# Maxima of an attention stage's first 256 tokens taken head group by head group, on one Trainium2 core

## What is computed

```python
mk, mv = split(mem @ Wkv.T)                       # keys and values of the gathered rows
logits = einsum('bhld,bmd->bhlm', q_heads, mk) / sqrt(8)
attn = softmax(logits, axis=-1)                   # per head h, token l, over rows m
out = einsum('bhlm,bmd->bhld', attn, mv)
x = x + tanh(g_xattn) * (out @ Wc.T)
```

## Time and profile before

| | us |
|---|---|
| median of three executions | 337.15 |
| lowest, highest | 333.48, 337.73 |
| the profiled execution | 335.67 |
| its span | 333.9 |

### The profile page before, as it was taken

How to read it: one execution, slowest core, us unless ns; L and a number is a source line. 1 busy time by engine, 2 the same in 40 slices (tenths; PEclk the granted TensorE clock), 3 DMA queues, 4 the chain that set the end, 5 groups by cost and what they waited for, 6 DMA issues and landing times.

```text
span 333.9 us, 5318 instructions
## 1 busy us (share of the span) xinstructions
PE 291.1 (87%) x1781; PEld 214.3 (64%) x1781; DVE 190.1 (57%) x686; ACT 155.5 (47%) x333; POOL 78.7 (24%) x165
## 2 busy tenths in 40 slices
PE   5899979999986778869999888998889997888993
PEld 2688979999985335547777666664333433357993
DVE  4585555766888777888787868220211206725344
ACT  1665543555543014757676667686314120045640
POOL 3873135465545422000000001000023000244000
PEclk9999997999999987999999999999999999689998
DMA  7832553656200000029180000100001000011002
GB/s 204 284 110 93 182 180 135 206 197 213 90 22 12 16 8 20 1 82 332 13 247 0 6 0 3 36 2 2 0 3 36 0 0 3 7 40 21 14 2 63
DMA packets 18459, 24.09 MB, mean 72 GB/s; under 512 B 2120, under 2 KB 14986, under 8 KB 18426
## 3 DMA queue, kind: packets, MB, share of 16 engines
q1 hardware_dynamic: 16836, 20.39, 18.3%
q0 software_dynamic: 1184, 3.14, 4.1%
q10 hardware_dynamic: 406, 0.16, 0.2%
HBM read 12.62 MB, written 10.93 MB: 71 GB/s over the span
## 4 chain that ended last, share of the span: by engine, by line
PE 59%; DVE 17%; DMA 8%; issue 6%; ACT 4%; POOL 4%; SPq 0%; DVEq 0%; ACTq 0%; POOLq 0%
PE ps L1417 8%; PE ps L1472 7%; PE ps L1526 6%; DVE mx L1093 4%; PE ps L1504 4%; PE ps L1365 4%; PE ps L1367 3%; PE ps L1366 3%; PE ps L1326 3%; PE ps L1644 3%; DMA pair<-in_ctx_dram,at 3%; PE ps L1650 3%; PE ps L1673 2%; PE ps L1412 2%; DVE kv_nat L1084 2%
## 5 line engine op out<-in xcount | busy, mean ns | idle before, releaser
L937 DVE CUSTOM_DVE_ANT_0 kv_nat<-ps,gain 128x400 f32<-128x400 f32 (+1 forms) x64 | 36.3, 573 | 22.1 <-PE ps L1367 19.8
L1365 PE MATMUL ps<-shared,q_hi 128*128 128x400 f32 (+1 forms) x128 | 46.9, 367 | 2.0 <-DVE best L937 1.2
L697 ACT ACTIVATE gain<-ps 128x400 f32<-128x400 f32 (+1 forms) x64 | 32.3, 505 | 32.5 <-PE ps L1367 32.2
L1093 DVE TENSOR_REDUCE mx<-ps 128x1 f32<-128x384 f32 x84 | 40.9, 546 | 9.6 <-PE ps L1504 9.5
L1367 PE MATMUL ps<-shared,q_lo 128*128 128x400 f32 (+1 forms) x128 | 44.8, 350 | 0.0
L1366 PE MATMUL ps<-shared,q_hi 128*128 128x400 f32 (+1 forms) x128 | 44.7, 349 | 0.0
L803 ACT ACTIVATE kv_nat<-ps 128x512 f32<-128x512 f32 x72 | 39.3, 602 | 9.0 <-PE ps L1526 8.2
L1526 PE MATMUL ps<-q_rows,k_blk 128*128 128x256 f32 x192 | 39.9, 300 | 2.6 <-DVE mx L1084 1.7
L1526 PEld LDWEIGHTS ps<-q_rows,k_blk 128*128 128x128 f32 x192 | 31.5, 190 | 8.0 <-issue 2.9
L1504 PE MATMUL ps<-k_blk,q_rows 128*128 128x384 f32 x84 | 28.5, 365 | 1.5 <-DVE mx L1093 1.4
L609 POOL TENSOR_TENSOR rstd<-var_eps,minus_half 128x4 f32<-128x4 f32 x2 | 2.1, 1032 | 114.1 <-DVE var_eps L1124 114.1
(11 more groups left out here) (297 smaller groups left out, 509.8 us busy)
## 6 DMA issues: line engine op xcount, KB each, us to landing
m_rows<-kv_nat SPq DMA_DIRECT2D x48, 201.0 KB, 2.1
kv_nat<-in_ctx_dram SPq DMA_DIRECT2D x5, 640.0 KB, 9.6
ew_sb<-in_L_ffn_eW_dram SPq DMA_DIRECT2D x1, 2048.0 KB, 10.2
rw_sb<-in_L_ffn_rW_dram SPq DMA_DIRECT2D x1, 1024.0 KB, 5.4
x_sb<-in_x_dram SPq DMA_DIRECT2D x2, 256.0 KB, 3.9
xn_rows<-xn SPq DMA_DIRECT2D x2, 256.0 KB, 2.3
out_dram<-fin SPq DMA_DIRECT2D x4, 128.0 KB, 1.9
rw_sb<-in_L_ffn_rW_dram SPq DMA_DIRECT2D x1, 256.0 KB, 2.9
```

What stands on the lines that cost most here:

```text
L697: act.activation(gain[:, m % 3, 0:end - start], ps[:, b:b + end - start], ACT.Relu).then_inc(s_rl, 1)
L937: dve.tensor_tensor_reduce(out=m_all[b2][:, start:end], in0=ps[:, b:b + end - start], in1=gain[:, m % 3, 0:end - start], scale=1.0, scalar ...
L1093: dve.tensor_reduce(to, sc, AX.X, ALU.max).then_inc(s_p1u, 1)
L1365: pe.matmul(o, q_h, hi, start=True, stop=False)
```

## The change

The list of jobs starts with the 32 heads of tiles 0 and 1 in order of head group: group 0 of both tiles, then group 1 and so on. Each group has a turn of its own: two transposes of four columns each, tiles 0 and 1, into one bank, two VectorE instructions over 4 partitions by 256 columns, and two DMAs that write 4 partitions' rows of one group into `q_rows`. The first logits of group g wait for the rows of group g alone (`s_nmgroup`). The opening holds 10 jobs: four rises of two heads (group 0), and the group's turn behind the first of five more rises of two heads. The rest of tiles 0 and 1 are rises of one head between the logits, and of the later tiles every third head (`(GH * g + j) % 3 == 2`) is too. A rise of one head keeps both products, 192 columns each, in one bank (`rise_1` has three slots). A turn waits only for the jobs whose maxima it turns, and stands behind two jobs of the next tile (one, for group 0).

There are 129 jobs: 9 rises with 18 heads in the opening, 44 rises of one head and 66 plain ones in the loop, 4 group turns and 6 tile turns. `jobs_at` now has a date for each quarter: all jobs up to its turn are spread over the first 10 of the 12 steps before that quarter, and the last two have none. So steps 0 to 9 have 53 jobs, 12 to 21 have 34, 24 to 33 have 32, and steps 10, 11, 22 and 23 none. The router's weight loads come behind the fourth group's rows, `ew1` behind the second quarter's rows and `ew2` behind the third's.

```diff
-LEAD = 5
+LEAD = 4
@@ program
+        nmg_hi = shared[0:GH, 3 * TOK:4 * TOK]
+        nmg_lo = shared[0:GH, 4 * TOK:5 * TOK]
+        rise_1 = kv_flat[:, 16 * W:16 * W + 3 * W].rearrange("p (b k) -> p b k", b=3)
@@ max_jobs
+            units = [(i, g, j) for g in range(NG) for i in range(TQ) for j in range(GH)]
+            units += [(i, g, j) for i in range(TQ, NT) for g in range(NG) for j in range(GH)]
+            first = 0
+            while units:
+                i, g, j = units[0]
+                key = -1 - g if i < TQ else i
+                w = together if first == 0 or len(jobs) < first + LEAD else 1
+                if jobs and key != owner:
+                    turn, mine = owner, 0
+                owner = key
+                jobs.append((i, (g, j, j + w)))
+                units, mine = units[w:], mine + 1
+                if turn is not None and mine == (1 if key == -2 else 2):
+                    jobs.append((turn, None))
+                    first = first or len(jobs)
+                    turn = None
@@ by_rise
-            return max_jobs(T)[m][1] is not None and m < opening_of(T)
+            i, unit = max_jobs(T)[m]
+            return unit is not None and (m < opening_of(T) or T <= 4 and (i < TQ or (GH * unit[0] + unit[1]) % 3 == 2))
@@ jobs_at
-            first, last = opening_of(T), (NQ - 1) * NG * T - 2
+            per, turns = NG * T, max_turns(T)
+            due = [opening_of(T)] + [turns[q] for q in range(1, NQ)]
...
-                return first + -(-(len(max_jobs(T)) - first) * min(x + 1, last) // last)
+                q, r = divmod(x + 1, per)
+                if q >= NQ - 1:
+                    return due[-1]
+                return due[q] + -(-(due[q + 1] - due[q]) * min(r, per - 2) // (per - 2))
@@ minus_max_rows (SyncE)
+                for g, done in enumerate(group_turns(T)):
+                    sp.wait_ge(s_p1u, done)
+                    for r, src in ((3 * DH, nmg_hi), (3 * DH + 1, nmg_lo)):
+                        sp.dma_start(q_rows[r:P:RS, g, 0:W].bitcast(F32), src[:, g * W:(g + 1) * W].bitcast(F32)
+                                     ).then_inc(s_nmgroup[g], 16)
@@ rise_of (ScalarE)
+                    elif by_rise(T, m):
+                        act.wait_ge(s_p1, m + 1)
+                        w, b = T * P // 2, job_bank(T, m) * HALF
+                        act.activation(rise_1[:, m % 3, 0:w], ps[:, b:b + w], ACT.Relu).then_inc(s_p1r, 1)
@@ max_job (VectorE)
+                    if unit is not None and by_rise(T, m) and m >= opening_of(T):
+                        dve.wait_ge(s_p1r, rises_before(T, m) + 1)
+                        g, j0, j1 = unit
+                        b = job_bank(T, m) * HALF + hk
+                        dve.tensor_tensor_reduce(out=rise_1[:, m % 3, 0:hk], in0=ps[:, b:b + hk], in1=rise_1[:, m % 3, 0:hk],
+                                                 scale=1.0, scalar=LOWEST, op0=ALU.add, op1=ALU.max,
+                                                 accum_out=mx[:, i, NG * j0 + g:NG * j0 + g + 1]).then_inc(s_p1u, 1)
...
+                    elif i < 0:
+                        c, b = slice((-1 - i) * W, -i * W), job_bank(T, m) * HALF
+                        link(dve.tensor_scalar(nmg_hi[:, c], ps[0:GH, b:b + W], -1.0, None, ALU.mult))
+                        dve.scalar_tensor_tensor(out=nmg_lo[:, c], in0=ps[0:GH, b:b + W], scalar=-1.0,
+                                                 in1=nmg_hi[:, c].bitcast(F32), op0=ALU.mult, op1=ALU.subtract
+                                                 ).then_inc(s_p1u, 1)
@@ max_job (TensorE)
-                        pe.wait_ge(s_p1u, m if m == len(jobs) - 1 else m - 1)
+                        pe.wait_ge(s_p1u, done_for(T, m))
+                        if i < 0:
+                            b = job_bank(T, m) * HALF
+                            for k in range(TQ):
+                                mine = mx[:, k, :].rearrange("p (j g) -> p j g", j=GH)[:, :, -1 - i]
+                                last = pe.transpose(ps[0:GH, b + k * P:b + (k + 1) * P], mine, ident[:])
+                            last.then_inc(s_p1, 1)
+                            return
...
+                    if by_rise(T, m) and m >= opening:
+                        b = job_bank(T, m) * HALF
+                        for k, keys in enumerate((kd_blk, k_blk)):
+                            last = pe.matmul(ps[:, b + k * hk:b + (k + 1) * hk], q_rows[:, g, i * P:(i + 1) * P],
+                                             keys[:, j0, 0:hk], start=True, stop=True)
+                        last.then_inc(s_p1, 1)
+                        return
@@ attention_pe
+                            if q == 0 and t == 0:
+                                pe.wait_ge(s_nmgroup[g], 32)
+                            elif s == 0:
                                 pe.wait_ge(s_nmrow[q], 32)
```

More of the change, by code:

```diff
@@ L285, in program @@
         s_p1 = sem("logits_for_max_ready"); s_p1u = sem("logits_for_max_used")
+        s_nmgroup = [sem(f"minus_max_row_of_group{g}") for g in range(NG)]
         s_nmrow = [sem(f"minus_max_row{L}") for L in range(NQ)]
@@ L331, in max_jobs, with done_for, group_turns @@
         def max_jobs(T):
[L334 to L343, removed]
-            return jobs + [(NT - 1, None)]
+            jobs, turn, mine, together = [], None, 0, 2 if T <= 4 else 1
+            units = [(i, g, j) for g in range(NG) for i in range(TQ) for j in range(GH)]
[14 more added lines that the diff above has]
+                    turn = None
+            return jobs + [(NT - 1, None)]
+        def done_for(T, m):
+            jobs = max_jobs(T)
+            i = jobs[m][0]
+            mine = [k for k, (tile, unit) in enumerate(jobs) if unit is not None and
+                    (tile == i if i >= 0 else tile < TQ and unit[0] == -1 - i)]
+            return max(mine) + 1
+        def group_turns(T):
+            return [max_jobs(T).index((-1 - g, None)) + 1 for g in range(NG)]
         def opening_of(T):
-            return max_turns(T)[0] + LEAD
+            return group_turns(T)[0] + LEAD
         def by_rise(T, m):
-            return max_jobs(T)[m][1] is not None and m < opening_of(T)
+            i, unit = max_jobs(T)[m]
+            return unit is not None and (m < opening_of(T) or T <= 4 and (i < TQ or (GH * unit[0] + unit[1]) % 3 == 2))
         def places(T, m):
@@ L376, in max_turns @@
             jobs = max_jobs(T)
-            return [jobs.index((TQ * (q + 1) - 1, None)) + 1 for q in range(NQ)]
+            return {q: jobs.index((TQ * (q + 1) - 1, None)) + 1 for q in range(1, NQ)}
         def jobs_at(T, step):
-            first, last = opening_of(T), (NQ - 1) * NG * T - 2
+            per, turns = NG * T, max_turns(T)
+            due = [opening_of(T)] + [turns[q] for q in range(1, NQ)]
             def upto(x):
-                return first + -(-(len(max_jobs(T)) - first) * min(x + 1, last) // last)
+                q, r = divmod(x + 1, per)
+                if q >= NQ - 1:
+                    return due[-1]
+                return due[q] + -(-(due[q + 1] - due[q]) * min(r, per - 2) // (per - 2))
             return range(0 if step < 0 else upto(step - 1), upto(step))
@@ L421, in _, with load_weights @@
                                  m_all[i % 2][:, c * STEP:c * STEP + CHUNK]).then_inc(s_mst[i], 16)
-            def minus_max_rows(T):
-                for q, done in enumerate(max_turns(T)):
+            def load_weights(q):
+                if q == 0:
+                    sp.dma_start(rw1_sb[:], rW1).then_inc(s_w, 16)
+                    sp.dma_start(rw2_sb[:], rW2.rearrange("(k p) n -> p k n", p=P)).then_inc(s_w, 16)
+                    sp.wait_ge(s_rz, 1)
+                    sp.dma_start(rw3_sb[:, :, 0:E], rW3.rearrange("(k p) n -> p k n", p=P)).then_inc(s_w, 16)
+                if q == 1:
+                    sp.dma_start(ew1_sb[:], eW1.rearrange("e c h -> c e h")).then_inc(s_w, 16)
+                if q == 2:
+                    sp.dma_start(ew2_sb[:], eW2.rearrange("e (k p) c -> p e k c", p=P)).then_inc(s_w, 16)
+            def minus_max_rows(T):
+                for g, done in enumerate(group_turns(T)):
[3 more added lines that the diff above has]
+                                     ).then_inc(s_nmgroup[g], 16)
+                load_weights(0)
+                for q, done in max_turns(T).items():
                     sp.wait_ge(s_p1u, done)
@@ L768, in rise_of @@
                 def rise_of(m):
-                    if by_rise(T, m):
+                    if by_rise(T, m) and m < opening_of(T):
                         act.wait_ge(s_p1d, rises_before(T, m) + 1)
@@ L1078, in max_job @@
                     dve.wait_ge(s_p1, m + 1)
-                    if unit is not None and by_rise(T, m):
+                    if unit is not None and by_rise(T, m) and m >= opening_of(T):
[5 more added lines that the diff above has]
+                                                 accum_out=mx[:, i, NG * j0 + g:NG * j0 + g + 1]).then_inc(s_p1u, 1)
```

(1 more changed line is left out.)

10 lines of the change are left out of this document (1 added, 9 removed).

## The result

The changed kernel takes 353.35 us (median of 4, 349.17 to 353.72) against 336.6 for the kernel before in the same runs: ratio 1.0529, 95% interval 1.0478 to 1.0581. The prediction was 339.4 us with a range up to 345.0. The direction was right and the size was not: 17 us slower instead of 3. All ratios here compare fast executions only, with executions of the kernel before that ran beside each set (its medians there were 335.7, 335.5 and 334.2 us), so a ratio can't be had by dividing two medians.

What follows compares the result with a forecast made beforehand. VectorE was taken to bound the loop and opening. Terms -7.6 + 10.9 - 1.4 + 2.1 - 0.9 = +3.1, say +3.0, on 335.67 gave 338.7; half the median's 1.5 excess made 339.4 us, range 334.5 to 345.0.

Steps and rivals of the forecast that it cites:

- its terms for the way over ScalarE: Loop rises: round trips take steps 0 to 3 to 11.0 us; in steps 4 to 9 each rise loses 0.1.
- The opening, -7.6: Before the first logits: 9 pairs and one turn instead of 22 and two, logits at 141.0 not 148.6 us.
- The term for the row DMAs: End of the opening: rows land 2.5 to 3.4 us behind the turn's last instruction, at 140.7 to 141.4.
- VectorE: 0.28 instead of 0.476: Loop: a rise of one head between logits takes VectorE 0.28 us, where a plain job takes 0.476.
- The round trip binds: Rival, chance 0.20: steps 0 to 3 take 12.2 us, each later rise loses 0.2; 344.0 or 344.7 us.
- 1.2 us of pause at a weighing: Loop stages: each takes its VectorE work plus 1.2 us of pause, with 4.1 as the floor.
- Steps 0 to 3, 11.0 forecast: First stage of the loop: 11.0 us instead of 6.5, +4.5, taken nearer to the round trip.
- the two bounds, 9.1 and 12.2: Steps 0 to 3: VectorE's work plus pause gives 9.1 us, the round trip of the rises gives 12.2.
- -1.4 for both: Steps 10 to 12 and 22 to 24: nearly the floor, 4.3 us instead of 5.0 each.
- +2.1 - 0.9: Steps 13 to 21 and 25 to 33: +2.1 us of VectorE work; six tile turns that wait less credit -0.9.
- Not slower: Rival, chance 0.25: round trip costs nothing, weighing pause is filled; steps 0 to 9 take 23.6 us, total 334.8 or 335.5.
- The prediction's last sign: Stages 13 to 33: if they also grow by more than 1 us each, the loop price of a rise is wrong.

Runs made afterwards that it cites:

- changed, clock kept: Changed kernel plus nine products of 512 columns into an unused bank while TensorE waits for the first group's rows; 349.83 us, ratio 1.0449.
- no loop rises, clock kept: Changed kernel with all jobs behind the opening plain, plus nine products into an unused bank before the first logits; 347.66 us, ratio 1.0377.
- 33 jobs: Kernel before with a longer opening, 30 pairs of heads and three turns instead of 22 and two; 332.5 us, ratio 0.9945.
- groups, long opening: Changed kernel's group order and group turns, but 22 pairs in the opening, no rises behind it, jobs spread evenly; 335.18 us, ratio 1.005.
- 29 jobs: Kernel before with a longer opening, 26 pairs of heads and three turns instead of 22 and two; 333.86 us, ratio 0.9984.

## Why the prediction was wrong

**How the 18.3 us divide.** By the sums of the tables: 93.91 (changed) to 91.26 (changed, clock kept) is 2.6 us for the clock; to 86.90 (no loop rises, clock kept) is 4.4 for the 44 rises; to 83.38 is 3.5 for 14 heads and two turns of the first block in the loop and not in the opening (that run had some half clock, so it is rather a little more); to 77.20 is 6.2 for the dates and for six more pairs, twelve heads, that belong in the opening (the expectation above says six heads); to 75.59 is 1.6 for the group turns. Dates alone were 4.6 on the kernel before, rises alone 4.8. The opening's 7.2 us are inside these net figures: steps 0 to 3 by themselves took 7.8 more than before.

**How the error of 15.2 us divides.** The forecast had +3.1 for this stretch. Put 0.476 for every 0.28 in its loop terms, take its terms for the way over ScalarE out, and it has +8.1 with all loop jobs plain; so it gave the rises -5.0. Measured at full clock, it is +11.3 with all jobs plain and +4.4 for the rises. That makes 9.4 us of error on the rises, 3.2 on the rest (1.9 of it in steps 10 to 12 and 22 to 24, below) and 2.6 on the clock. So the step that failed is the price of a rise between logits, on VectorE and behind a weighing.

**The opening, -7.6: right.** Measured -7.2. The term for the row DMAs had 2.5 to 3.4 us and they took 3.1. (From 145.38 to 148.60 it is 3.2; the 3.4 is a slip, and the 141.4 worked out with 3.2 is right.) The logits came at 139.66 and not at 141.0, mainly because this execution's first rise was 1.8 us earlier (131.71, 133.47 before).

**"VectorE: 0.28 instead of 0.476" for a rise between logits: wrong, and the largest error.** The figure was read where 44 heads follow each other in pairs. Between reductions a rise takes 0.45 (one and two plain jobs every 1.40 us). The forecast counted a way of 0.82 us for a rise against 0.96 for the two plain jobs before it. The rows have 0.98, from the products at 157.32 to VectorE at 158.30. And these products could not be issued earlier: with three banks and every third job a rise, TensorE waits for VectorE to leave the rise before (156.90 to 157.18), 0.14 us ahead of them. 0.28 + 0.14 + 0.98 = 1.40, so the way sets the pace. Its other parts were priced well (a Relu of 192 columns took 0.33 us, 0.32 forecast). The rival "The round trip binds" let a rise lose 0.2. On the kernel before, 26 rises alone cost 4.8 us, where the forecast's prices would have made them some 5 us cheaper than plain jobs: an error of 10 us on an isolated part, and of much the same kind here.

**"1.2 us of pause at a weighing": a constant that was not one.** It holds with plain jobs, as VectorE's timeline of the run with the later tiles plain shows:

```profile
154.34 3.81 DVE L1142 TENSOR_REDUCE mx<-ps 128x1 f32<-128x384 f32 x8 [1.18 <-PE ps L1573]
```

With a rise at the head of the stage it is 2.06, because logits, exponential and Relu come before VectorE's first work. The forecast put such rises at 0.1.

**Steps 0 to 3, 11.0 forecast and 14.3 measured.** The forecast's 11.0 runs to the end of the weighing, so it has to be set beside 139.66 to 153.94, 14.28 us. Of the 3.3 missing, 1.45 are the half clock. With the clock kept the same stretch took 12.84, still above the forecast and above the upper one of the two bounds, 9.1 and 12.2. So the round trip's bound was nearer, and itself 0.6 short. Without rises and with the clock kept it took 12.42, bound by VectorE: the 15 rises, credited with 0.2 us of VectorE each, gained nothing. A part of it is the group turn, forecast at 0.6 us of VectorE; its two instructions take 0.41 us each.

**Steps 10 to 12 and 22 to 24, "-1.4 for both": wrong sign, +2.4.** I took the floor of stages without jobs. The timeline of the changed kernel:

```profile
171.35 0.28 DVE L1153 SCALAR_TENSOR_TENSOR shared<-ps,shared 16x128 fp32r<-16x128 f32 x1
...
171.66 1.13 SPq L474 DMA_DIRECT2D q_rows<-shared  x2
...
174.14 0.50 PE L1597 MATMUL ps<-q_rows,k_blk 128*128 128x256 f32 x2 [0.40 <-DMA q_rows<-shared]
...
175.70 0.36 DVE L1125 CUSTOM_DVE_ANT_0 kv_nat<-ps,kv_nat 128x192 f32<-128x192 f32 x1 [4.07 <-ACT kv_nat L815]
```

The turn of tile 3 ended at 171.63 and its rows were there 2.5 us later, which I had covered with 2.8 us for steps 10 and 11. These began at 171.99 and left TensorE standing for 0.40 us at the end. That is the small part. VectorE stands for 4.07 us and then has all four jobs of step 12 in front of the weighing. The kernel before with the new dates alone, whose rows were in time, took 4.93 us for these stages, a gain of 0.1 for both and not 1.2, where stages with five or six evenly spread jobs took 4.27: the place of the four jobs costs the rest. In the changed kernel's 6.24, 0.35 more come from the late rows (5.28 without rises, clock kept), 0.7 from the rises (5.96 with them) and 0.3 from the half clock.

**Steps 13 to 33 (without 22 to 24), "+2.1 - 0.9": +7.3.** With all jobs plain they are +4.7. The model explains that: 54 plain jobs and four turns there are 54 x 0.476 + 4 x 0.6 = 28.1 us of VectorE against 22.9 before, +5.2. What the forecast had subtracted is 16 x 0.2 for the rises, and that never came; the rises add a further 1.3, and the second clock dip 1.3. The credit of 0.9 for turns that wait less is at most the 0.5 between 5.2 and 4.7.

**The rivals.** "The round trip binds" was the nearest, with its mechanism and place; its 344.7 was 8.6 us short, since it took over the dates' credit (-1.4, measured +2.4) and had no clock. "Not slower" rested on rises that bring banks back sooner; both pairs of runs that differ by rises alone refute it (+4.4 and +4.8 us). The prediction's last sign, stages 13 to 33 growing by over 1 us each, stood for a wrong price of a rise. They grew by 0.4 to 2.6 us, but by 4.7 of their 7.3 even with plain jobs, so that sign could not tell the price from the load.

## What to carry over

A job's price belongs to its neighbours: the same instruction took 0.28 us in a row of its own kind and 0.45 between reductions, so read a price where the job will stand, and count the way over every engine that it crosses against the number of buffers. When an engine bounds a stretch, moving its work to an earlier start gains nothing unless that work is as cheap in the new place; here the cheap form (pairs, in the opening) was shortened to start the dear form sooner, and going the other way gained 0.55%. And idle steps of the bounding engine gave back next to nothing here (0.1 us of 1.2), whatever was spread evenly around them.

## What the runs showed of the hardware

In the changed kernel TensorE's clock fell from 2.4 to 1.2 GHz at 142.0 us, after the engine had been idle for 2.5 us before the first logits and for 0.54 behind them (to 141.59). It stayed there until 148.8, 6.8 us, with the engine busy for 6.14 us of the window of 6.20 shown. Nine products of 512 columns in the wait kept it at 2.4 GHz, in both kernels that had them. Shorter waits before the first logits went either way: 1.70 us and no half clock in the kernel before and with 33 jobs; 1.69 us and 3.4 us of half clock in "groups, long opening"; 1.28 us with 29 jobs, in which the clock fell and stayed half for 6.8 us. I had not expected that of kernels that differ by four jobs, and what decides it is open.

Two DMAs of 4 rows by 256 columns were there no sooner than two of 16 rows: 3.1 us behind the turn's last instruction, against 2.5 for tile 3's turn here and in the earlier trace rows, and at most 3.2 in the earlier trace rows.
